# A cross-attention and expert-choice FFN kernel on one core: reordered start and last body, shorter search rounds, lists in chunks, first units in column halves

## The reference

```python
x = x + xattn(layernorm(x), ctx)          # x, ctx: 16 x 256 x 256, one head, D = 256
h = layernorm(x).reshape(4096, 256)
S = sigmoid(h @ Wg).T                     # 8 experts
G, I = top_k(S, 1024)                     # each expert picks its 1024 tokens
hid = gelu(h[I] @ W1 + b1)                # 256 -> 1024
out = (hid @ W2 + b2) * G                 # 1024 -> 256
x = x + scatter_add(out at I)
```

## Time and profile before

| | us |
|---|---|
| median of 3 runs | 547.64 |
| the profiled execution, whole | 549.17 |
| its span, first to last instruction | 547.4 |
| busy in the span: PE / DVE / ACT / POOL | 491.1 / 332.0 / 307.8 / 293.2 |
| bodies | 20.5 to 143 |
| search, lists, gather | 143 to 192.8 |
| experts | 192.8 to the end |
| mean granted TensorE clock | 0.944 |

### The profile page before, as it was taken

How to read it: one execution, slowest core, us unless ns; L and a number is a source line. 1 busy time by engine, 2 the same in 40 slices (tenths; PEclk the granted TensorE clock), 3 DMA queues, 4 the chain that set the end, 5 groups by cost and what they waited for, 6 DMA issues and landing times.

```text
span 547.4 us, 10408 instructions
## 1 busy us (share of the span) xinstructions
PE 491.1 (90%) x3671; PEld 351.6 (64%) x3671; DVE 332.0 (61%) x739; ACT 307.8 (56%) x562; POOL 293.2 (54%) x436
## 2 busy tenths in 40 slices
PE   4999999998523299999999999999999999999995
PEld 3777777777411245864874884794685586486484
DVE  7477777876588847547538538546645654733720
ACT  3666666654534059249439519727826925935921
POOL 5736998893600416734653671671672763555055
PEclk9999999998655589999999999999999999999998
DMA  7312555545195155943862771771782593484024
GB/s 237 107 46 69 153 147 134 137 131 150 38 275 157 41 130 172 171 72 127 141 121 76 156 144 27 200 149 19 195 162 29 152 180 55 136 126 49 0 31 50
DMA packets 91929, 64.19 MB, mean 117 GB/s; under 512 B 53044, under 2 KB 87800, under 8 KB 91896
## 3 DMA queue, kind: packets, MB, share of 16 engines
q1 hardware_dynamic: 79248, 46.42, 31.1%
q0 software_dynamic: 12288, 17.05, 18.8%
q10 hardware_dynamic: 360, 0.30, 0.2%
HBM read 35.83 MB, written 16.91 MB: 96 GB/s over the span
## 4 chain that ended last, share of the span: by engine, by line
PE 59%; issue 6%; DVE 5%; POOL 4%; DMA 2%; SPq 2%; ACT 1%; POOLq 0%; DVEq 0%; ACTq 0%
PE bank L1026 54%; PE bank L1257 3%; POOL out L460 2%; DVE junk L794 2%; SPq L266 2%; POOL xrow L387 1%; DMA out<-yo,ids_s 1%; DMA rows_d<-xrow 1%; POOL ex L447 1%; DVE thr L815 1%; PE bank L1233 1%; DMA ex<-rows_d,ids 1%; DMA yo<-xrow 0%; DVE oneh L907 0%; POOL xrow L379 0%
## 5 line engine op out<-in xcount | busy, mean ns | idle before, releaser
L1026 PE MATMUL bank<-w2h,xres 128*128 128x256 f16 x1024 | 169.0, 273 | 0.0
L1026 PE MATMUL bank<-exT,w1h 128*128 128x512 f16 x512 | 153.3, 381 | 0.6 <-DVE exT L1012 0.6
L1026 PE MATMUL bank<-w2l,xres 128*128 128x256 f16 x512 | 139.7, 273 | 0.0
L967 DVE TENSOR_TENSOR xres<-g,xres 128x512 f16<-128x512 f32 x128 | 87.6, 690 | 60.4 <-ACT xres L598 60.4
L460 POOL DMA_INDIRECT out<-yo,ids_s x64 | 101.0, 1577 | 25.6 <-issue 24.9
L1026 PEld LDWEIGHTS bank<-w2h,xres 128*128 128x128 f16 x1024 | 100.1, 98 | 12.5
L594 ACT ACTIVATE g<-bank,b1e 128x512 f32<-128x512 f32 x128 | 88.0, 688 | 25.4 <-PE bank L1026 20.3
L611 ACT ACTIVATE yo<-yt,ge 128x256 f32<-128x256 f32 x64 | 32.5, 508 | 119.5 <-DVE yt L981 119.5
L1026 PE MATMUL bank<-exT,w1l 128*128 128x512 f16 x256 | 97.7, 381 | 0.0
L1026 PEld LDWEIGHTS bank<-exT,w1h 128*128 128x128 f16 x512 | 49.8, 98 | 59.5 <-issue 1.4
L598 ACT ACTIVATE xres<-bank,b1e 128x512 f16<-128x512 f32 x128 | 87.2, 681 | 0.0
(11 more groups left out here) (215 smaller groups left out, 779.7 us busy)
## 6 DMA issues: line engine op xcount, KB each, us to landing
w1r<-in_L_ffn_W SPq DMA_DIRECT2D x8, 1024.0 KB, 6.6
w2r<-in_L_ffn_W SPq DMA_DIRECT2D x8, 1024.0 KB, 5.3
ctx<-in_ctx SPq DMA_DIRECT2D x8, 512.0 KB, 5.0
xres<-in_x SPq DMA_DIRECT2D x8, 512.0 KB, 5.9
rows_d<-xrow SPq DMA_DIRECT2D x8, 512.0 KB, 3.5
out<-xres SPq DMA_DIRECT2D x4, 1024.0 KB, 9.1
b_bc<-in_L_ffn_b SPq DMA_DIRECT2D x8, 128.0 KB, 4.5
ex<-rows_d,ids POOLq DMA_INDIRECT x64, 3.8
```

The costliest lines, as they stand in the source:

```text
L967: dve.tensor_tensor(hid[1][:, f, h * 512:(h + 1) * 512], g32[:, u % 2, :], hid[0][:, f, h * 512:(h + 1) * 512], ALU.subtract).then_inc(s[" ...
L1026: last = pe.matmul(out, lhs(a, c), rhs(b, c), start=i == 0, stop=i == len(terms) - 1)
```

## The change

- **Start.** 24 and 14 matmuls without use of their result (`keep_awake`) stand before the Wq transposes and behind the bias transpose. The second pair of ctx and x loads waits until the first ctx is there. Wg comes on ACT's queue. The small products and their DVE operations stand behind the first `project_v`. The search tables are smaller, and POOL fills them behind `add_bv(0)`.
- **Bodies.** On DVE `x1_stats` moves behind `cTl` and `row_max`. W1 is loaded in body 3 and W2 in body 6 (6 and 7 before); ACT splits W1's high part in bodies 5 and 6. In body 7 V's parts come before P's on ACT and DVE.
- **Last bodies.** `late_router` is cut in halves, the first half of group 6 ahead of `router(5)`, its second behind group 7. ACT loads the sigmoid table in body 8. The keys' sigmoid comes before the gates'.
- **Search.** DVE's thresholds no longer exist: the base accumulates (`gain[:, b, 3:4]`), the counting instruction subtracts it itself, and the instruction that compares the counts with K adds up the new base. ACT forms its own threshold (`thr3`) in each round. W1's low part is made in eight pieces in rounds 3 to 6 and 8 to 11.
- **Lists and first units.** A one-hot instruction now makes all 128 places of 8 tiles, and PE starts on each quarter as it is there. 16 more `keep_awake` matmuls, then list 1, row transposes and the first column halves of units 0 to 3 (`early_unit`) are interleaved.

```diff
# SP
             for i in range(2):
+                if i:
+                    sp.wait_ge(LD_C[0], landed(0))
                 sp.dma_start(ctx[:, i], cv[:, i * TP:(i + 1) * TP, :]).then_inc(LD_C[i], 16)
...
+                if k == 3:
+                    sp.dma_start(w1r[:, :, :], w1_d[0].rearrange("(c p) f -> p c f", p=P)).then_inc(s["ld_w1"], 16)
                 if k == NP - 2:
-                    sp.dma_start(w1r[:, :, :], w1_d[0].rearrange("(c p) f -> p c f", p=P)).then_inc(s["ld_w1"], 16)
-                if k == NP - 1:
                     sp.dma_start(w2r[:, :, :], w2_d[0].rearrange("(c p) f -> p c f", p=P)).then_inc(s["ld_w2"], 16)
# POOL, behind add_bv(0) and ident16
+            for r in range(ROUNDS):
+                pool.memset(gain[:, r + r // HI_ROUNDS, 0:3], STEP[r])
+                pool.memset(apart12[:, r, 0:1], STEP[r])
+                pool.memset(apart12[:, r, 1:2], 2.0 * STEP[r])
...
# ACT, body
+                if n == NP - 1:
+                    evict_v(n)
                 if runs(n, k, 1):
...
+                if n in (NP - 3, NP - 2):
+                    act.wait_ge(s["ld_w1"], 16)
+                    w1_hi(0, n - (NP - 3))
                 if k >= NP:
                     x1_evict(n - 2)
+                    if n == NP:
+                        act.activation(act_tick[:], eps[:, 0:1], ACT.Sigmoid)
                     apply_ln2(n - 2)
# ACT, search round
+                act.activation(thr3[:, r % 2:r % 2 + 1], gain[:, b, 3:4], ACT.Identity, bias=upto3[:, r:r + 1]).then_inc(s["thr3_s"], 1)
...
+                act.wait_ge(s["thr3_s"], r + 1)
...
+                    act.activation(asign[:], khi[:] if r < HI_ROUNDS else krel[:], ACT.Sign, bias=thr3[:, r % 2:r % 2 + 1], scale=-1.0,
                                    accum_out=cnt[:, 2:3]).then_inc(s["srch_act"], 1)
# DVE, body
-                    if n < NP:
-                        for h in range(2):
-                            x1_stats(h)
                 if runs(n, k, -1):
                     lo(cT[1][:], B_[:], cT[0][:], "c_hi", n + 2, "c_lo", XS)
                 if runs(n, k, 0) and n < NP - 1:
                     row_max()
+                if runs(n, k, 1):
+                    for h in range(2):
+                        x1_stats(h)
# DVE, search round
-                    dve.tensor_scalar(junk[:, c], keys[:], thr[:, c:c + 1], None, ALU.is_ge, ALU.add,
-                                      accum_out=cnt[:, c:c + 1]).then_inc(s["srch_cmp"], 1)
+                    dve.scalar_tensor_tensor(junk[:, c], keys[:], gain[:, b, 3:4], apart12[:, r, c:c + 1].unsqueeze(2).broadcast_to([P, 2, P]),
+                                             ALU.subtract, ALU.is_ge, accum_out=cnt[:, c:c + 1]).then_inc(s["srch_cmp"], 1)
...
+                dve.scalar_tensor_tensor(passed[:], A_[:, 1, 0:4], float(K), gain[:, b, :], ALU.is_ge, ALU.mult,
+                                         accum_out=gain[:, b + 1, 3:4]).then_inc(s["thr_s"], 1)
# DVE, one-hots
-                dve.tensor_tensor(oneh[:, k0:k1, :], iota16[:, k0:k1, :], lo_e[:, :].unsqueeze(1).broadcast_to([P, k1 - k0, NT]),
+                part = slice(NT // HOTS * j, NT // HOTS * (j + 1))
+                dve.tensor_tensor(oneh[:, :, part], iota16[:, :, part], lo_e[:, part].unsqueeze(1).broadcast_to([P, P, NT // HOTS]),
                                   ALU.is_equal).then_inc(s["hot_s"], 1)
# PE
+            def keep_awake(out, moving, times):
+                for _ in range(times):
+                    pe.matmul(out, before16[:], moving, start=True, stop=True)
...
+            def early_unit(f, q):
+                cols = slice(q * 256, (q + 1) * 256)
+                return pairs(bank[f // 2][:, f % 2, cols], lambda a, c: w1[a][:, c, f * P:(f + 1) * P],
+                             lambda b, c: exT[:, DC * b + c, cols], DC)
```

More of the change, by code:

```diff
@@ L63, in build @@
     KEEP = 5
-    SPLIT = 1
+    EARLY = 4
     ST_X1 = 4
@@ L545, in body @@
                     apply_ln1(n + 1)
-                if runs(n, k, 0) and k != 0:
+                if runs(n, k, 0) and 0 < n < NP - 1:
                     evict_v(n)
@@ L566, in _ @@
             phase_a(body)
-            act.wait_ge(s["l_ev"], NP)
-            act.activation(gate[:], logit[:], ACT.Sigmoid, scale=1.0 / (XS * AS)).then_inc(s["gate_r"], 1)
             act.wait_ge(s["key_tr"], 1)
@@ L576, in _ @@
                 if r == HI_ROUNDS:
-                    act.wait_ge(s["krel2_s"], 1)
+                    act.wait_ge(s["krel_s"], 1)
+                act.wait_ge(s["thr3_s"], r + 1)
                 with nc.allow_low_precision(reason="sums of 256 signs are whole numbers of at most 256"):
-                    act.activation(asign[:], khi[:] if r < HI_ROUNDS else krel[:], ACT.Sign, bias=thr[:, 2:3],
+                    act.activation(asign[:], khi[:] if r < HI_ROUNDS else krel[:], ACT.Sign, bias=thr3[:, r % 2:r % 2 + 1], scale=-1.0,
                                    accum_out=cnt[:, 2:3]).then_inc(s["srch_act"], 1)
+                if r == 1:
+                    act.wait_ge(s["kint_s"], 2)
+                    act.activation(klo[:], C_[:, 1, 0:2 * P].bitcast(I32).rearrange("p (a b) -> p a b", a=2), ACT.Copy,
+                                   scale=1.0 / (1 << LO_BITS)).then_inc(s["klo_s"], 1)
             act.activation(act_tick[:], eps[:, 0:1], ACT.Gelu)
-            act.wait_ge(s["ld_w1"], 16)
-            for c in range(DC):
-                w1_hi(0, c)
             def layer1(e, first):
@@ L963, in expert @@
                     h, f = u // FC, u % FC
-                    if first and u == SPLIT:
-                        read_list(1, False, C_)
                     dve.wait_ge(s["h_hi"], 2 * FC * e + u + 1)
@@ L1192, in body @@
                     x1_transposes(LAST)
+                    late_router(LAST, 0)
                 if 0 <= n - 3 < LAST:
@@ L1204, in body @@
                     transpose_x(n)
-                if k == 0:
-                    pe.wait_ge(s["ld_wg"], 16)
-                    pe.wait_ge(s["const1"], 6)
-                    for d in range(DC):
-                        last = pe.matmul(A_[:, 1, 0:E], onesf[:], wg[:, d, :], start=d == 0, stop=d == DC - 1)
-                    last.then_inc(s["u_mm"], 1)
                 if n == NP:
                     x1_transposes(LAST + 1)
-                    late_router(LAST)
-                    late_router(LAST + 1)
+                    late_router(LAST + 1, 0)
+                    late_router(LAST + 1, 1)
+                    late_router(LAST, 1)
             phase_a(body)
@@ L1286, in expert @@
                     list_of(e + 2, False)
-            pe.wait_ge(s["l_ev"], NP)
             list_of(0, True)
+            keep_awake(C_[:, 1, 0:2 * P], iota16[:].rearrange("p a t -> p (a t)")[:, 0:2 * P], 16)
             pe.wait_ge(s["id_ev"], 1)
             pe.wait_ge(s["ident16_s"], 1)
-            for t in range(KT // 2):
-                pe.wait_ge(s[f"gat_{t}"], 16)
-                for c in range(4):
-                    last = pe.transpose(rowT16[t][:, c * P:(c + 1) * P], ex16[:, t, c * P:(c + 1) * P], ident16[:])
-                last.then_inc(s["ex_tr"], 1)
+            list_part(1, 0)
+            list_part(1, 1)
+            row_transposes(0)
+            list_part(1, 2)
+            row_transposes(1)
+            list_part(1, 3)
+            pe.wait_ge(s["w1_lo_s"], 4)
+            pe.wait_ge(s["ex0_act"], 1)
+            pe.wait_ge(s["ex0_dve"], 1)
+            early_unit(0, 0)
+            row_transposes(2)
+            early_unit(1, 0)
+            row_transposes(3)
+            for f in range(2, EARLY):
+                early_unit(f, 0)
+            pe.wait_ge(s["ex0_act"], 2)
+            pe.wait_ge(s["ex0_dve"], 2)
             expert(0, True, True, True)
```

241 lines of the change are left out of this document (118 added, 123 removed).

## The result

The changed kernel takes 540.17 us (median of 4 runs, 539.56 to 541.24) against 548.01 us before (median of 4, 547.56 to 549.37): ratio 0.9855, 95% interval 0.9831 to 0.9879, a gain of 7.8 us. It is faster, as forecast, and inside the range, but 3.9 us above the forecast of 536.3. The two profiled executions are 549.17 and 539.98, their spans 547.4 and 538.2: 9.2 us apart. `kth_q` holds the 1024th largest gates, and `ids` the row numbers that the gather reads.

A forecast was written before the change was run, and what follows sets the result against it. The prediction took PE and POOL as nearly full in the bodies and PE as only serving from the keys to expert 0; 2.7 + 2.4 - 0.5 + 2.4 + 4.3 = 11.3 us off 549.17, median 536.3, range 531.5 to 541.5.

The forecast's parts named there:

- start: Before the first body: V starts at 12.8 and `project_g(0)` at 17.8 instead of 20.46, a gain of 2.7 us.
- bodies: In the bodies: `x1_stats` behind `row_max` removes POOL's waits for statistics, a gain of 2.4 us, bounds 0 and 3.0.
- last bodies: Before the keys: order saves 1.5 us, but PE's longer wait before `router(5)` drops the clock, costing 2.0; net -0.5.
- search: Search for the K-th gate: rounds of 1.53 us, 1.59 with W1's pieces, instead of 1.63; a gain of 2.4 us.
- lists and first units: Expert 0's list 1.5 us sooner, and early half units during the gather; together a gain of 4.3 us.
- rival E: At the start: the clock stays low, so V gains 1.4 instead of 2.7 us; 537.6 us, chance 0.12.
- the statistics themselves end no later against PE: Step for the bodies: DVE's sum of work is unchanged, so moving `x1_stats` does not delay statistics relative to PE.
- Rival B: Bodies and search rounds keep their length, bound by POOL and DVE, or ACT in the search; 541.0 us, chance 0.2.
- Rival A: The clock stays up in both waits, before `router(5)` and in the gather: +2.0 and +1.8; 532.5 us, chance 0.2.
- rival D: In the search: the new count runs in several passes, at three 20 us more; 557.4 us, chance 0.03.
- rival C: In the lists: one-hots run at half rate, each of two lists 2.2 us later; 540.7 us, chance 0.05.
- which I take to be untouched: Experts after 197.23: PE runs on without a gap worth naming and the change leaves that part as it is.

The follow-up runs named there:

- stats_before: The changed kernel with `x1_stats` back at its old place on VectorE, as before the change; ratio 0.9861 to the kernel before.
- hold_router5: The changed kernel with 26 matmuls nobody reads in PE's wait before `router(5)`; ratio 0.9804 to the kernel before.
- tail: `attend_first` with POOL's rstd of the last tile ahead of a cast and `late_router(6)`'s second half ahead of `late_router(7)`; 531.65 us, ratio 0.9715.
- list_late: The changed kernel with expert 1's whole list, and VectorE's reading of it, moved behind the four early half units; ratio 0.9849 to the kernel before.
- attend_first: The changed kernel with `attend(8)` ahead of `router(5)` on PE and `router(5)`'s logit reduction behind both `x1_stats` on VectorE; 535.5 us, ratio 0.9776.
- psum_steps: The changed kernel with the search's count steps copied once to PSUM and read from there; ratio 0.981 to the kernel before.
- t2_first: The changed kernel with the transposes of rows 2 and 3 put ahead of early units 0 and 1; ratio 0.9855 to the kernel before.
- best: `tail` with count steps in PSUM, expert 1's list behind the second halves and 21 instead of 16 `keep_awake` matmuls; ratio 0.9719 to the kernel before.
- whole_units: `list_late` with the list behind unit 3 and the first four units whole, behind all four rows' transposes; ratio 0.9885 to the kernel before.
- tail_psum: `tail` with the count steps in PSUM and nothing else; ratio 0.9722 to the kernel before.

## Why the prediction was right, and where its sizes were off

The terms, forecast against measured (by the table above): start 2.7, measured 3.0; bodies 2.4, measured 1.7; last bodies -0.5, measured -1.05; search 2.4, measured 2.9; lists and first units 4.3, measured 3.6; behind layer 1 nothing, measured -0.9. The sum, 11.3, came out at 9.2.

**Start.** The size is right, and rival E is out: the first batch of 24 matmuls took 2.74 us, the eight transposes behind it 1.23 instead of 1.94, and the second batch of 14 took 0.95, so the clock was up before 7 us, with transposes between the batches. My reason against E, that these 24 are denser work than what stood there before, was weak: they take 2.74 us, and the 12 products with as many columns in all took 2.77. V went at 2.4 GHz from its first matmul and took 2.6 us, as forecast. But the two batches were not what carried the gain: without them `project_g(0)` is 0.47 later.

**Bodies.** I let all of POOL's waits go; two stayed. The step that failed is "the statistics themselves end no later against PE": in two of the four bodies they still ended too late for POOL, by 0.34 and 0.22. Rival B is out, since the pitch did fall. And of the 2.5 us that this order gave PE in the bodies, 1.05 went into the wait before `router(5)` and 0.8 into the low clock behind it, so that 0.65 reached the keys (`stats_before`).

**Last bodies.** The wait before `router(5)` was forecast at 3.1 and is 3.04, the fall of the clock behind it as well. Its cost was taken as 2.0 inside 1.8 to 2.9; it is 2.5 in `attend`, and 2.25 at the keys by `hold_router5`. Rival A's first half is out, and so is its second: in the gather the 16 matmuls of `keep_awake` took 3.57 us, which is 1.2 GHz, and the clock rose only at 186. That the wait is a matter of order alone I had not seen: `attend` never needed the rows.

**Search.** A round is 1.44, not 1.53 or 1.59: ScalarE's matmul is at 0.98 as forecast, but the last one follows 0.04 behind it, and `passed` stands at 1.23 instead of 1.30; W1's pieces fit in. Rounds 1 to 3 took 1.51, 2.03 and 2.24, 1.46 more than three at 1.44. "The new counts have one more operand; I price one at the old 0.40 pitch" is right while POOL rests and wrong while it works. A dearer count was there for three rounds, but not by rival D's mechanism of several passes, since the same instruction goes at 0.41 in the other rounds.

**Lists and first units.** The list 1.5 sooner: measured 1.47, and one-hots at 2.49 for four, so rival C is out. The first units gave 2.1 instead of 2.8: the second halves stood 13.33 us behind `ids`, where the forecast's 194.3 was 12.7. In `tail`, with the same order here, they stood 11.11 behind, as its evictions were prompt.

**Experts "which I take to be untouched".** They were not, by the 0.82 us that PE waits for the first `yt`. VectorE was not late with its own work: its last piece of layer 1 ended at 209.62, PE's first tile of layer 2 at about 209.2, and `yt` started only at 212.27, after 2.65 idle us. It starts 5.74 us behind the start of layer 2, in the kernel before and in `tail` 2.82. All nine kernels with late evictions have it late, 4.8 to 6.0 us, but in six of them the trace shows no wait of PE for it; `list_late` has it at 4.18 with prompt evictions. So the 0.8 comes and goes between kernels, and in `hold_router5`, `attend_first` and `psum_steps` it is a part of the gain in time.

**From execution to median.** 1.7 of the 3.9 us are no mechanism: I took 1.5 off because the profiled execution of before lay above its median; that of the changed kernel lies 0.2 below its own.

**Open.** It is open why the evictions are late. In nine kernels the second one on ACT comes 12.63 to 12.71 us behind `ids`, whatever PE's order (`t2_first` included); in `tail`, `list_late`, `best` and `whole_units` 7.7 to 8.6. Without the list's pieces between the rows it was prompt three times of three, with them once in ten. No trace names what ACT and VectorE wait for. The rows have one coincidence that no run tested: in all nine the late eviction starts 1.21 to 1.28 us behind the end of POOL's last gather instruction (186.47 in the changed kernel), and the late `yt`, less tightly, 0.8 to 1.5 us behind the end of the last one of the second gather (211.02). In the four prompt kernels the evictions come 2.8 us and more ahead of that end. A run with the gather cut short or moved would tell whether it is the cause.

## What to carry to other kernels

Ask of a wait first whether the waiting instruction has to stand there: moving `attend` past a router that waited for a DMA gave 4.3 us and filling the wait with matmuls 2.8, while of the 2.5 us by which the earlier bodies let PE come to that wait sooner, 0.65 reached the keys. Where the order in the source is the order on the engine, it is worth trying to put a short instruction that others wait for ahead of one that waits for a transfer; in `tail` that, with one more move, gave 1.93 us at the keys. And a gain should be followed through the next stages: the 1.5 and 1.2 us of the search in `best` and `tail_psum` were spent before layer 2. A last one: a wait of 0.8 us that comes and goes elsewhere can make an experiment look better than its cause, so compare places in the trace and not only times.
